# Second attention: squares and lengths of queries and keys by halving additions on GpSimd, and the stack copy one square sooner on VectorE

## The reference, cut to what matters

```python
q2 = jnp.sum(Q * Q, axis=-1, keepdims=True)
k2 = jnp.sum(K * K, axis=-1, keepdims=True)
sq = q2 + jnp.swapaxes(k2, -1, -2) - 2.0 * jnp.einsum('bhqd,bhkd->bhqk', Q, K)
dist = jnp.sqrt(jnp.maximum(sq, 0.0))
W = (SHEP_EPS + dist) ** (-SHEP_P)
W = W / (SHEP_EPS + jnp.sum(W, axis=-1, keepdims=True))
return jnp.einsum('bhqk,bhkd->bhqd', W, V)
```

## Time and profile before

| | |
|---|---|
| median of 3 runs | 4124.66 us (4123.56 to 4129.85) |
| the profiled execution | 4136.65 us, its span 4134.9 us |
| PE, PEld busy | 3544.1 us (86%), 2571.6 us (62%) |
| DVE busy | 2524.1 us (61%) |
| ACT busy | 2219.4 us (54%) |
| POOL busy | 1042.4 us (25%) |

### The profile page before, as it was taken

One profiled execution on the slowest core, in us unless ns is written; L12 is line 12 of the kernel. 1 busy time (PEld: TensorE's weight loads), 2 busy tenths in 40 slices (PEclk: granted clock), 3 DMA queues, 4 the chain that ended last, 5 costly groups with the idle time before them and its releaser, 6 DMA issues. The chain is left out here.

```text
span 4134.9 us, 55565 instructions
## 1 busy us (share of the span) xinstructions
PE 3544.1 (86%) x21924; PEld 2571.6 (62%) x21924; DVE 2524.1 (61%) x3838; ACT 2219.4 (54%) x2873; POOL 1042.4 (25%) x922
## 2 busy tenths in 40 slices
PE   5788888887999999997776777777766999999998
PEld 3445444444888889997333333333323888889998
DVE  4555555554443335654799999999996443335564
ACT  1454545554332224442799898899895432224443
POOL 3321323210002210212455263272330002210121
PEclk7889999999999999998787877878877999999999
DMA  3000000001001012342000000000001001012332
GB/s 117 1 1 1 1 1 1 1 1 62 6 9 43 23 48 86 91 119 64 17 1 1 1 1 1 1 1 1 1 1 62 6 6 41 28 48 80 94 91 53
DMA packets 86804, 124.91 MB, mean 30 GB/s; under 512 B 7767, under 2 KB 73257, under 8 KB 86544
## 3 DMA queue, kind: packets, MB, share of 16 engines
q1 hardware_dynamic: 68880, 100.18, 7.1%
q0 software_dynamic: 17664, 21.17, 3.1%
HBM read 85.15 MB, written 42.55 MB: 31 GB/s over the span
## 5 line engine op out<-in xcount | busy, mean ns | idle before, releaser
L487 DVE TENSOR_REDUCE a_mxp<-a_deep 128x1 f32<-128x512 f32 (+3 forms) x768 | 391.8, 552 | 363.1 <-PE a_deep L667 299.1
L1817 DVE TENSOR_TENSOR b_w<-b_w 128x2048 f32<-128x2048 f32 x256 | 583.3, 2309 | 22.9 <-ACT b_w L1895 14.7
L1854 ACT ACTIVATE b_w<-b_ring 128x1024 f32<-128x1024 f32 x512 | 482.0, 1049 | 97.2 <-PE b_ring L1937 96.9
L1895 ACT ACTIVATE b_w<-b_w 128x2048 f32<-128x2048 f32 x256 | 468.0, 1897 | 1.4
L1367 ACT ACTIVATE f1hid<-f1ring 128x512 f32<-128x512 f32 (+2 forms) x256 | 132.3, 517 | 577.4 <-PE f1ring L1447 560.4
L1367 ACT ACTIVATE f2hid<-f2ring 128x512 f32<-128x512 f32 (+2 forms) x256 | 132.3, 517 | 577.0 <-PE f2ring L1447 560.0
L1925 PE MATMUL b_acc<-b_w,b_vg 128*32 128x512 f32 x2048 | 324.5, 715 | 129.6 <-DVE b_w L1817 128.9
L586 ACT ACTIVATE a_prob<-a_wide 128x1024 f32<-128x1024 f32 (+1 forms) x320 | 294.4, 943 | 242.5 <-PE a_wide L697 163.1
L1285 DVE TENSOR_TENSOR f1hid<-f1hid,f1ring 128x512 f32<-128x512 f32 (+2 forms) x256 | 150.1, 586 | 440.2 <-ACT f1hid L1367 440.1
L1285 DVE TENSOR_TENSOR f2hid<-f2hid,f2ring 128x512 f32<-128x512 f32 (+2 forms) x256 | 150.0, 586 | 439.4 <-ACT f2hid L1367 439.3
L1761 DVE TENSOR_SCALAR b_w<-b_w 128x2048 f32<-128x2048 f32 x256 | 324.7, 1313 | 34.4 <-ACT b_w L1854 34.0
(11 more groups left out here) (340 smaller groups left out, 6831.0 us busy)
## 6 DMA issues: line engine op xcount, KB each, us to landing
X<-expert_in SPq DMA_DIRECT2D x16, 650.0 KB, 5.1
expert_in<-a_zeros SPq DMA_DIRECT2D x8, 650.0 KB, 10.4
X<-in_x SPq DMA_DIRECT2D x4, 1024.0 KB, 10.2
x_mid<-X SPq DMA_DIRECT2D x8, 512.0 KB, 3.2
f1raw_x<-in_rd SPq DMA_DIRECT2D x4, 1024.0 KB
f1raw_xf<-in_rg SPq DMA_DIRECT2D x4, 1024.0 KB, 4.9
f1raw_xf<-in_ru SPq DMA_DIRECT2D x4, 1024.0 KB, 7.0
f1raw_g<-in_rg SPq DMA_DIRECT2D x4, 1024.0 KB, 4.8
```

The source lines that it names most:

```text
L487: v.tensor_reduce(mxp[:, t, 2 * e + h, i:i + 1], dslot(step, h)[:, 0:n], AX_X, ALU.max).then_inc(s_dve, 1)
L1817: v.tensor_tensor(one(m), one(m), one(m), ALU.mult).then_inc(s_wts, 1)
L1854: s.activation(w[:, m, 2 * pair:2 * pair + 2, :].rearrange("p h n -> p (h n)"), slot(at + pair), ACT.Ln, scale=SHEP_EPS ** -2).then_inc(R. ...
L1895: s.activation(one(m), one(m), ACT.Sigmoid, scale=-0.5).then_inc(s_sig, 1)
```

## The change

Three things are edited, all in `attention_b`. ACT's squares (`squared`) and DVE's sums (`lengths`) are taken out, with their two semaphores. POOL gets its own `lengths(n)`, ahead of the four builds of the unit. For each half of the tokens it multiplies queries and keys by themselves into `square`, and adds the upper half of each group of 16 to the lower, then 8 to 4, 4 to 2, and the last pair into `len2`; a drain of POOL stands between the steps. It waits for `s_qk`, the same signal of DVE's `take` that ACT waited for. And on DVE, `operand(n, m)` now stands ahead of the wait for sigmoid m and of the square of m, in place of behind them.

```diff
--- before.py
+++ after.py
@@ -1576,8 +1576,6 @@
         s_xn = sem("b_xn_ready")
         s_xnT = sem("b_xnT_ready")
         s_qk = sem("b_qk_ready")
-        s_square = sem("b_qk_squared")
-        s_len = sem("b_lengths_ready")
         s_vg = sem("b_values_ready")
         s_stack = sem("b_stack_ready")
         s_qkT = sem("b_stack_transposed")
@@ -1643,6 +1641,22 @@
                     pool.tensor_tensor(xs, xs, b_out[:].unsqueeze(1).to_broadcast([P, TB, D]), ALU.add)
                     pool.drain().then_inc(s_xadd, 1)
 
+                def lengths(n):
+
+                    for x in range(2):
+                        half = slice(x * TILES, (x + 1) * TILES)
+                        mine = qk[:, half].rearrange("p t h a d -> p (t h a) d")
+                        squares = square[:, x].rearrange("p t h a d -> p (t h a) d")
+                        pool.wait_ge(s_qk, 2 * n + x + 1)
+                        pool.tensor_tensor(squares, mine, mine, ALU.mult)
+                        pool.drain()
+                        for d in (8, 4, 2):
+                            pool.tensor_tensor(squares[:, :, 0:d], squares[:, :, 0:d], squares[:, :, d:2 * d], ALU.add)
+                            pool.drain()
+                        sums = len2[:, half].rearrange("p t h a -> p (t h a)").unsqueeze(2)
+                        pool.tensor_tensor(sums, squares[:, :, 0:1], squares[:, :, 1:2], ALU.add)
+                    pool.drain()
+
                 def build(n, i):
 
                     e, side = STACKS[i]
@@ -1651,7 +1665,6 @@
                     norm = len2[:, :, heads, side:side + 1]
                     st = stacks[:, i].rearrange("p t (h n) -> p t h n", h=2)
                     hi2, lo, at = (DH, 2 * DH, 3 * DH + 2) if side else (2 * DH, DH, 3 * DH)
-                    pool.wait_ge(s_len, 2 * n + 2)
                     if n:
 
                         pool.wait_ge(s_qkT, len(STACKS) * (n - 1) + i + 1)
@@ -1673,6 +1686,7 @@
                 pool.memset(vg[:, :, :, :, DH:DH + 1], 1.0)
                 pool.drain().then_inc(s_init, 1)
                 roots(0)
+                lengths(0)
                 for i in range(len(STACKS)):
                     build(0, i)
                 pool.wait_ge(s_w, WLOADS)
@@ -1681,6 +1695,7 @@
                     b, p = divmod(j, TB)
                     n = j // 2 + 1
                     if j % 2 == 0 and n < UNITS:
+                        lengths(n)
                         for i in range(len(STACKS)):
                             build(n, i)
                     if b + 1 < B:
@@ -1738,15 +1753,6 @@
                                     bias[:, :, :, 3 * DH:4 * DH].to_broadcast([P, TILES, HG, DH]), ALU.add
                                     ).then_inc(R.free[at % SLOTS], 1)
 
-                def lengths(n, x):
-
-                    dve.wait_ge(s_square, 2 * n + x + 1)
-                    if n:
-                        dve.wait_ge(s_stack, len(STACKS) * n)
-                    mine = len2[:, x * TILES:(x + 1) * TILES]
-                    v.tensor_reduce(mine.rearrange("p t h a -> p (t h a)"),
-                                    square[:, x].rearrange("p t h a d -> p (t h a) d"), AX_X, ALU.add).then_inc(s_len, 1)
-
                 def operand(n, i):
 
                     at = AT["stack", n, i]
@@ -1802,7 +1808,6 @@
                 dve.wait_ge(s_init, 1)
                 for x in range(2):
                     take(0, x)
-                    lengths(0, x)
                 for i in range(len(STACKS)):
                     operand(0, i)
                 for m in range(TB):
@@ -1813,16 +1818,14 @@
                         gates(j - 1)
                     n = j // 2 + 1
                     for m in range(TB):
+                        if j % 2 and n < UNITS and m < len(STACKS):
+                            operand(n, m)
                         dve.wait_ge(s_sig, TB * j + m + 1)
                         v.tensor_tensor(one(m), one(m), one(m), ALU.mult).then_inc(s_wts, 1)
                         if n < UNITS:
                             if j % 2 == 0:
                                 if m < 2:
                                     take(n, m)
-                                if m in (4, 5):
-                                    lengths(n, m - 4)
-                            elif m < len(STACKS):
-                                operand(n, m)
                         if b and p < 2 and m == 6:
                             add(b - 1, p)
                     for m in range(TB if j + 1 < PERIODS else 0):
@@ -1870,20 +1873,9 @@
                     s.copy(xn[:, 0:TILES, :].rearrange("p t d -> p (t d)"), slot(at)).then_inc(R.free[at % SLOTS], 1)
                     act.drain().then_inc(s_oTT, 1)
 
-                def squared(n, x):
-
-                    act.wait_ge(s_qk, 2 * n + x + 1)
-                    if n:
-                        act.wait_ge(s_len, 2 * n)
-                    s.activation(square[:, x].rearrange("p t h a d -> p (t h a d)"),
-                                 qk[:, x * TILES:(x + 1) * TILES].rearrange("p t h a d -> p (t h a d)"), ACT.Square
-                                 ).then_inc(s_square, 1)
-
                 s.preload_act_table_set("natural_log")
                 for x in range(2):
                     tokens(0, x)
-                for x in range(2):
-                    squared(0, x)
                 for m in range(TB):
                     log(0, m)
                 for j in range(PERIODS):
@@ -1893,8 +1885,6 @@
                     for m in range(TB):
                         act.wait_ge(s_bound, TB * j + m + 1)
                         s.activation(one(m), one(m), ACT.Sigmoid, scale=-0.5).then_inc(s_sig, 1)
-                        if j % 2 == 0 and n < UNITS and m in (4, 6):
-                            squared(n, m // 2 - 2)
                         if p == 4 and b + 1 < B and m in (5, 7):
                             tokens(b + 1, m // 2 - 2)
                         if p < 2 and b and m == 4:
```

## The result

| | median us | against the kernel before |
|---|---|---|
| before | 4129.85 (5 runs, 4123.56 to 4137.19) | |
| changed | 4163.50 (5 runs, 4157.69 to 4173.58) | 1.0083, 95% interval 1.0067 to 1.0099 |

The change makes the kernel 34 us slower. The forecast was 4209 us in a range of 4145 to 4255: the sign is right and the time is inside the range, but the loss is less than half of the 84 us forecast. Rival A, to which I had given a chance of 0.17, had 4156.

The account below looks back on a forecast made before the run. DVE was taken to set the odd period's end, ACT and DVE nearly level in the even. 59 + 26 - 3 + 2.5 = 84.5 us on the median 4124.7 gave 4209 us, range 4145 to 4255.

Parts of the forecast that it names:

- Rival A: POOL gets in at every DVE boundary; holds cost DVE 1.5 us a plain pair, +31 us, 4156 us; chance 0.17.
- the port is closed for six squares and four bounds: Even period: DVE's back-to-back SBUF instructions shut POOL out, so its seven late instructions wait until about L1766, 3055.8 us.
- 5.0 us of waiting for stack 0, 2.0 for stack 3: Plain odd period: first stack copy starts 5.0 us late behind POOL's lengths and build; stack 3 adds 2.0 us.
- +59 us for nine plain pairs: Plain pairs of periods: 5.0 + 2.0 + 0.6 of holds - 1.0 = 6.6 us each, nine times.
- The 9.13 us: POOL's first copy of stack 0 in the loop, standing through five DVE boundaries; 0.40 us before the loop.
- 1.0 us of credit: Each plain pair: taken off the loss because POOL sometimes slips in between DVE's instructions, one or two times.
- Behind a residual: Three pairs: POOL's lengths queue after the residual, square 0's place 7.9 us late plus 0.6 of holds, +26 us.
- Start of a batch and before the loop: Three pairs at a batch's start gain 1 us each, -3 us; the second half before the loop adds 2.5 us.
- What is taken out: ACT squares and DVE sums removed: gain of 0 to 1.04 us in each of 15 even periods, at most 16 us.
- Period 30: Even period without `take`, ACT squares or sums, still 33.75 us; basis for the lower bound of no gain.
- The price of the ten instructions: POOL's added lengths in each unit: 3.6 us a half, 7.2 us a unit; 8.4 by the upper slope.
- The stack copies: First copy ahead of square 0 uses DVE's idle 0.67 us in twelve odd periods, 8 us at best.

Follow-up runs that it names:

- lengths-only kernel: The changed kernel with the stack copies (`operand`) back behind the squares, lengths staying on POOL: 4169.0 us, 1.0092 of the kernel before.
- the copies alone: The kernel before with only the stack copies' move (`operand(n, m)` ahead of the wait): 4124.74 us, ratio 0.9999.
- the kernel without lengths: The kernel before with ACT squares and DVE sums left out, no POOL additions, lengths kept constant, copies in place: 4117.33 us against 4125.31, ratio 0.9983.

## Why the prediction was wrong

The failed step is this one: "Then the port is closed for six squares and four bounds." From it came 5.0 us of waiting for stack 0, 2.0 for stack 3 and +59 us for nine plain pairs. Measured are +13.6 us, 9.3 in even and 4.3 in odd periods. There was no waiting for stack 0 in a plain pair and none for stack 3: POOL's ten instructions were let in one by one and were over in the second bound, and in the even periods the loss is what they hold DVE's squares.

- **The evidence was one observation.** The 9.13 us stand in nine units of the loop, at the same phase each time, and I took them for a rule. A small copy took the same 9 us in their place. At a batch's start the same copy after the same idle time took 2.39. Most of POOL's other instructions under DVE's runs were let in at the first or second boundary already in the trace of before, as in the 6.89 us of the earlier trace rows; I gave those 1.0 us of credit. The average of 1.6 us an addition is what being let in at nearly each boundary costs POOL.
- **Rival A names the mechanism, and its number is partly luck.** Squares of 2.3 to 3.1 us in even periods and no idle time ahead of the copy are the signs that the forecast gave for it. It gave 1.5 us a plain pair, by holds of DVE; measured is 13.6 / 9 = 1.5. But its 3.3 us of holds a period were 2.2 (eight squares of an even period take 20.42 us instead of 18.25), which less the 1.2 us of sums gives the +1.0 of the even periods, where it had +2.2; and in the odd ones, where it had -0.7, there are +0.5, which the lengths-only kernel does not have. Two misses cancel.
- **Behind a residual** the mechanism and the size were right: 23.1 us against 26. Counted from the first sigmoid of period 12, the residual ends 2.2 us later than before (forecast 1.3), and the first copy starts 6.8 us after the place of square 0 before (forecast 7.9). Moving the residual away removed the loss.
- **Start of a batch and before the loop**: -2.7 against -3, and +3.2 against +2.5. The first agrees by luck: the lengths alone cost 2.3 us there, and the copies' move gave 5.0 back.
- **What is taken out** was costed at 0 to 1.04 us an even period; 0.84 was there, and POOL's instructions in the same period took it and 1.0 more. Period 30 was a poor witness: it takes 31.9 to 34.0 us in the kernels traced here, though no edit touches what it does.
- **The price of the ten instructions** was near: 7.2 us alone was forecast and 8.3 measured behind a residual, where the first five still run beside the last bound. The second five run alone and take 3.5 us, against 3.6 forecast for a half.
- **The stack copies** were given 8 us at best if stack 0 is there. It was there, and nothing came. In the changed kernel's plain odd periods square 7 ends at 25.3 us after the first sigmoid, as before. With the copies alone, square 7 ends at 24.8 us in seven of the nine. In the changed kernel that half microsecond is lost ahead of the first copy, which starts 1.7 us after the first sigmoid instead of 1.2, since POOL holds the bounds too. The rest is lost behind it. Stack 2 is late for its copy by 0.4 us, and behind the squares PE runs more slowly. PE's granted clock in 10 us from 18 us after the first sigmoid on, in period 27 of the kernel before, then in period 7 of the changed one:

```profile
3010.74:3020.74 10.00, 7.14 (x50) 2.01 (x50) 10.00 (x7) 7.78 (x10) 0.00 (x0) 1.00 0.00 0
```

```profile
2279.16:2289.16 10.00, 9.75 (x56) 2.68 (x52) 10.00 (x7) 7.58 (x9) 0.00 (x0) 0.76 0.01 2
```

Before, the clock is 1.00 there in all nine plain odd periods, which is the higher of its two levels, 2.4 GHz, throughout. Period 7 of the changed kernel takes 36.70 us, with the clock at 0.76, and period 29 takes 35.79, with 0.83. The clock also falls where no copy was moved. In period 15 of the kernel without lengths the stretch holds the same 50 matmuls as before, and PE is busy with them for 8.99 us instead of 7.14:

```profile
2553.18:2563.18 10.00, 8.99 (x50) 2.37 (x50) 10.00 (x7) 7.10 (x9) 0.00 (x0) 0.75 0.01 2
```

That period takes 36.33 us; those of the same kernel with 1.00 there take 35.71. So the move of the copies is not what the fall needs, and what brings it about is open. No run here changed the clock alone, so its part in the odd periods' time is argued, not shown. It is not the whole of it either: with the copies alone, periods 3 and 27 take 37.32 us because DVE waits 2.21 us for PE's transposition of the last stack, which no other plain period of that kernel does:

```profile
2997.07 1.23 DVE L1755 CAST b_kT<-b_ring 128x1024 fp32r<-128x1024 f32 x1 [2.21 <-PE b_ring L1970]
```

In the forecast I had set aside one reading of the Trainium skill, "SBUF — State Buffer", section "SBUF: two separate sides": that of its exclusive lock the one who asked first is next. Read so, it has POOL let in at each boundary, as the changed kernel's rows show for the ten instructions. That a square takes 2.69 us instead of 2.28 beside POOL's product agrees with the lock. The stand of 9 us does not fit that reading.

## What to carry to other kernels

A stall that repeats at the same phase of a loop is one observation, however often it stands in the trace; look for the same instruction at other phases before it becomes a rule. Work moved to POOL beside back-to-back DVE instructions on SBUF is paid twice in these traces: POOL needs about one DVE instruction for each of its own, however small (2.10 us for 32 elements beside squares of 2.3), and DVE is held for nearly as long as a POOL instruction of two inputs takes alone (0.84 us of 1.04 for the product). Small additions hold DVE little but are slow on POOL, so a chain of them is late for whatever stands behind it. And on an engine with a long task in its list, ask what is queued behind that task: here three places out of fifteen made two thirds of the loss.

## What the runs showed that I had not expected

- In nine plain units of fifteen, POOL's first reading instruction after idle time stood through five boundaries of DVE, 8.93 to 9.13 us, whether it was 0.2 or 0.4 us of work; at a batch's start, after the same idle time, it took 2.18 to 2.39 us. Why it stands stays open.
- One POOL addition of 128 x 2048 in four places costs the kernel 0.3%: it holds a DVE bound of 1.22 us for 4 us more, and moving it only moves that.
- PE's granted clock in one stretch of the odd periods is 1.00 in each of nine before the change and 0.76 to 0.89 after it, with the same instructions in PE's list. It also falls in kernels where the copies stayed.
